# A decoder layer on one core: quad 3's exponentials moved ahead of the third keys on ScalarE, and a wait of GpSimd for the normalised x1

## The reference, cut to what matters

```python
x = x + self_attn(layernorm(x))           # the sum is x1
q = layernorm(x1) @ Wq.T                  # 16 heads of 64
k, v = ctx @ Wk.T, ctx @ Wv.T
probs = softmax(q @ k.T + mask)           # per head, 128 x 128
x = x + (probs @ v) @ Wo.T                # the sum is x2
x = x + ffn(layernorm(x))
```

## Time and profile before

| | us |
|---|---|
| median of 3 runs | 1637.55 (1637.49 to 1640.61) |
| the profiled execution | 1638.86 |
| its span, first to last instruction | 1637.1 |
| TensorE busy | 1522.7 (93%) |
| VectorE busy | 1427.2 (87%) |
| ScalarE busy | 1218.9 (74%) |
| GpSimd busy | 1067.1 (65%) |

### The profile page before, as it was taken

One profiled execution on the slowest core, in us unless ns is written; L12 is line 12 of the kernel. 1 busy time (PEld: TensorE's weight loads), 2 busy tenths in 40 slices (PEclk: granted clock), 3 DMA queues, 4 the chain that ended last, 5 costly groups with the idle time before them and its releaser, 6 DMA issues.

```text
span 1637.1 us, 52303 instructions
## 1 busy us (share of the span) xinstructions
PE 1522.7 (93%) x15938; PEld 1221.6 (75%) x15946; DVE 1427.2 (87%) x6188; ACT 1218.9 (74%) x2497; POOL 1067.1 (65%) x1168
## 2 busy tenths in 40 slices
PE   6589999999999999999999999999999999779897
PEld 5468888888888888888888888888888887532465
DVE  4779999999999999999999999999999996669786
ACT  4767777777777777777777777777777777469875
POOL 3467777777777777777777777777777777642000
PEclk9889999999999999999999999999999999889999
DMA  6000000000000000000000000000000000245154
GB/s 215 4 15 30 29 29 29 29 24 26 29 29 29 29 29 29 29 29 28 23 28 29 29 24 28 29 29 29 29 29 29 29 22 17 91 119 138 39 180 168
DMA packets 92292, 74.67 MB, mean 46 GB/s; under 512 B 20832, under 2 KB 91744, under 8 KB 92256
## 3 DMA queue, kind: packets, MB, share of 16 engines
q1 hardware_dynamic: 91296, 74.08, 14.7%
q10 hardware_dynamic: 960, 0.13, 0.1%
HBM read 45.36 MB, written 25.17 MB: 43 GB/s over the span
## 4 chain that ended last, share of the span: by engine, by line
PE 59%; DVE 18%; ACT 10%; issue 8%; POOL 3%; ACTq 1%; DVEq 1%; DMA 0%; POOLq 0%; SPq 0%
PE banks L124 16%; PE banks L127 13%; PE banks L128 12%; PE banks L914 5%; DVE tile_max L2126 4%; PE banks L934 3%; DVE xn L1342 2%; ACT kv_copy L1154 2%; PE banks L958 2%; ACT normed L1191 2%; PE banks L2030 2%; PE banks L806 2%; DVE g_t_half L1363 2%; DVE stats L1507 1%; POOL rstd L671 1%
## 5 line engine op out<-in xcount | busy, mean ns | idle before, releaser
L658 POOL TENSOR_TENSOR exp_t<-exp_copy,exp_t 128x512 f16<-128x512 f32 x256 | 303.4, 1185 | 141.9 <-ACT exp_copy L1176 82.8
L652 POOL TENSOR_TENSOR shifted<-scores,score_max 128x512 f32<-128x512 f32 x256 | 266.3, 1046 | 131.9 <-DVE score_max L1387 127.2
L1387 DVE CUSTOM_DVE_ANT_0 scores<-banks,mask 128x128 f32<-128x128 f32 x1024 | 232.7, 286 | 6.2 <-PE banks L914 2.9
L1151 ACT ACTIVATE q_t<-banks 128x512 f16<-128x512 f32 x128 | 77.2, 603 | 131.9 <-PE banks L128 131.7
L644 POOL TENSOR_TENSOR v_nat<-kv_copy,v_nat 128x512 f16<-128x512 f32 x128 | 143.8, 1123 | 46.1 <-ACT kv_copy L1154 46.0
L934 PE MATMUL banks<-ident,shifted 128*128 128x128 f32 x1024 | 153.6, 278 | 19.2 <-ACT exp_copy L1176 17.5
L1174 ACT ACTIVATE exp_t<-banks 128x512 f16<-128x512 f32 x256 | 153.6, 600 | 18.5 <-PE banks L934 15.6
L1176 ACT ACTIVATE exp_copy<-banks 128x512 f32<-128x512 f32 x256 | 156.1, 610 | 0.0
L1154 ACT ACTIVATE kv_copy<-banks 128x512 f32<-128x512 f32 x252 | 150.2, 596 | 0.0
L644 POOL TENSOR_TENSOR k_t<-kv_copy,k_t 128x512 f16<-128x512 f32 x124 | 143.9, 1161 | 0.0
L934 PEld LDWEIGHTS banks<-ident,shifted 128*128 128x128 f32 x1024 | 115.3, 142 | 27.6 <-issue 20.6
(11 more groups left out here) (276 smaller groups left out, 5059.3 us busy)
## 6 DMA issues: line engine op xcount, KB each, us to landing
x_in<-in_x_dram SPq DMA_DIRECT2D x32, 256.0 KB, 2.6
ctx_in<-in_ctx_dram SPq DMA_DIRECT2D x32, 256.0 KB, 2.6
x_residual<-x SPq DMA_DIRECT2D x64, 128.0 KB, 1.7
x_normalised<-normed SPq DMA_DIRECT2D x32, 256.0 KB, 2.1
shared<-x_normalised SPq DMA_DIRECT2D x8, 1024.0 KB, 6.9
shared<-x_residual SPq DMA_DIRECT2D x16, 512.0 KB, 3.7
out_dram<-shared SPq DMA_DIRECT2D x16, 512.0 KB, 2.9
mask<-in_fside_Bx1xSxS_dram SPq DMA_DIRECT2D x64, 64.0 KB, 1.9
```

The lines of the kernel that those rows point to most:

```text
L652: pool.tensor_tensor(shifted[:, q % 2], scores[:, q % 2], score_max[:, q % 2, :].unsqueeze(2).to_broadcast([P, QUAD, P]), ALU.subtract).th ...
L658: pool.tensor_tensor(exp_t[:, q % 2, LO], exp_copy[:, q % 2], exp_t[:, q % 2, HI], ALU.subtract).then_inc(exp_split, 1)
L1151: op = act.activation(hilo(dst, *at)[HI], src, ACT.Copy)
L1387: op = dve.tensor_tensor_reduce(scores[:, q % 2, h, :], sc_bank(q)[:, tile(h)], mask[:, b, :], 1.0, NEG, ALU.add, ALU.max, score_max[:, q ...
```

## The change

Two edits. On ScalarE `exponential(3)` of the pair before is called ahead of `hi(J_K2)` instead of behind it. On GpSimd a wait for `xn1_ready` of this pair is put between `shift(6)` and `exp_lo(5)`, in trips that have both `back` and `front`.

```diff
@@ gpsimd body
             if back:
                 shift(6, i - 1)
+                if front:
+
+                    pool.wait_ge(xn1_ready, i + 1)
                 exp_lo(5, i - 1)
                 shift(7, i - 1)
             if front and not early:
@@ scalar body
             if early:
                 weights_of["cross_hi"](act, 8, 12)
+            if back:
+                exponential(3, i - 1)
             if front and not early:
                 hi(J_K2, i)
             if back:
-                exponential(3, i - 1)
                 heads_hi(0, i - 1)
                 exponential(4, i - 1)
```

## The result

The changed kernel takes 1658.58 us (median, 1658.04 to 1658.96) against 1638.11 before, ratio 1.012 with a 95% interval of 1.0105 to 1.0135: slower by 20 us, where 23 were forecast (1660.5). The execution profiled has a span of 1656.9, against 1637.1.

The account below looks back on a forecast made before the run. TensorE bounds the loop, busy 41.04 of 42.07 us a trip. About +0.8 us over 30 trips (+24), less about 0.7 in trip 31, gives +23 on the 1637.55 median: 1660.5 us, range 1615 to 1672.

Parts of the forecast that it names:

- Part 1 (a): Quad 3's exponentials fit ScalarE's idle time at no cost; quad 5's transposes start earlier and could end a 0.37 us wait.
- Part 1 (b): GpSimd's `exp_lo(3)` and `lo(J_K1)` start earlier and hold VectorE's normalisation of `x_in`, making VectorE 1.48 us late.
- The transposes of xn: On TensorE, they wait for VectorE's late normalisation of `x_in` and start 1.3 us later.
- weigh(4)'s 0.28: On TensorE, weigh(4)'s 0.28 us delay, put down to `exp_lo(4)`, comes back because `exp_lo(4)` ends earlier.
- Part 2: GpSimd's wait before `exp_lo(5)` lets `x1`'s two normalisations run free in 0.73 us, giving 1.1 us back on VectorE.
- The sum: At the raw scores: +1.3 - 0.28 - 0.41 + 0.17, about +0.8 us a trip, +24 us over 30 trips.
- the wait for `g_t_half`: TensorE's wait before the raw scores would be gone, giving back 0.41 us a trip.
- The end: In trip 31 no `x_in` is normalised, so both edits give what they promise, about 0.7 us.
- Rival A: `x_in`'s normalisation is not held; TensorE wins 0.37 and 0.34 a trip, -22 us, 1616; chance 0.22.
- Rival B: Only the first normalisation of `x_in` is held, VectorE 0.65 late; about no change, 1634 to 1642; chance 0.13.
- Rival C: Held as forecast, and GpSimd's wait also ends after weigh(5) is due: +1.2 a trip, 1674; chance 0.13.

Follow-up runs that it names:

- e3: Changed kernel plus a GpSimd wait for `xn_ready` before `exp_lo(3)`, so it starts only after `x_in` is normalised: 1636.11 us.
- e5: Changed kernel plus a GpSimd wait for `xn_ready` between `exp_lo(3)` and `lo(J_K1)`: 1633.43 us.
- e4: Changed kernel without GpSimd's wait for `xn1_ready`, both normalisations with an unread accumulator output, product with `rstd` left out: 1618.41 us.
- e1: Changed kernel without GpSimd's wait for `xn1_ready`, so only ScalarE's `exponential(3)` is moved: 1655.24 us.
- e2: Kernel before with only GpSimd's wait for `xn1_ready` added, ScalarE's order as before: 1628.09 us.
- e8: Repeat of e2 on another chip, the kernel before with only GpSimd's wait for `xn1_ready`: 1627.63 us.
- e6: Kernel before, neither edit made, both normalisations in the accumulating form, product with `rstd` left out: 1622.63 us.

## Why the prediction was right

**Part 1 (a), no cost on ScalarE:** right; the third keys' time in the trip is unmoved.

**Part 1 (b), the normalisation of x_in is held:** right, and it was the deciding step. Forecast 1.48 us late on VectorE; the pair grew from 0.73 to 2.18, so 1.45. It is shown by e3 (take GpSimd away and the loss is gone), by e5 (take away one of two, and the wait falls from 1.68 to 0.85) and by e4 (leave GpSimd where it is and change the form). The rows that carried it were those of the twin instruction, the one on `x1`.

**The transposes of xn:** forecast +1.3, measured +1.33. **weigh(4)'s 0.28** came back as forecast: it starts 0.11 behind its predecessor, with `exp_lo(4)` ended two microseconds earlier. Another 0.04 was lost at the fourth keys, so the net is 0.23.

**Part 2:** the end of `x1`'s normalisation was put at 13.73 us after the second keys and came at 13.77; `exp_lo(5)` at 13.83, and came at 13.85. But the ground given for it was half wrong. I credited the wait with 1.1 us on VectorE; e1 has nearly the same pair (0.71 us) without it, since `exp_copy(5)` comes too late for GpSimd to be in the way. In this kernel the wait costs 0.09 us a trip. That the forecast of this part came out right in spite of it is luck: the pair is free with and without the wait.

**The sum:** +0.8 a trip forecast, +0.73 measured. weigh(5) came 0.07 later than I had it (15.15 against 15.08) and the raw scores followed 0.37 behind it, where I had allowed 0.47 and a rest. So the wait for `g_t_half` gave back 0.51 and not 0.41, and the fourth keys and weigh(4) 0.23 and not 0.28. The end won 1.2 us where I had 0.7, and not because both edits pay there: part 1 alone wins 1.7 (e1), part 2 alone loses 0.4 and 0.6 (e2, e8). 30 x 0.73 - 1.2 = 20.7, and 20.5 was measured.

**Rival A was mis-sized.** It gave part 1 the full 0.37 a trip. The rows spoke against that: `xn` is ready at 825.37, the transposes behind the waiting ones started at 825.64, so some 0.2 was there at best; e3 has them 0.13 earlier, and e4 against e6 shows 0 in a slower form. Rival B did not come, since both instructions were held; e5 made the case that it describes, and gave 41.95 where I had about 42.06. Rival C did not come: weigh(5) was 0.14 later than weigh(4) accounts for.

## What to carry to other kernels

Before an engine's work is moved into an idle gap, look at what runs beside that gap on the engine that it shares something with; a twin of the same instruction elsewhere in the trace, with the neighbour active, tells the price. A wait in front of the critical one is worth only as much as the next input of the same queue is early. And two edits that are each judged by the old order have to be measured one by one: here one lost 17 us, the other won 10, and together they lost 20. The wait was worth 10 us in the old order and cost 3 in the new one.

## What the runs showed of the hardware

With an accumulator output the VectorE instruction took 0.53 us instead of 0.405 and was never held (128 of 128 in e4); its second operation, the product, was missing from what it wrote. A GpSimd subtraction that starts during a VectorE normalisation loses about 0.1 us itself (1.26 in e1 and 1.29 before, against 1.16), while a normalisation of the usual form that starts during one loses up to 0.84 in the loop (1.24 against 0.405).
